# One stage for a row-wise linear layer and the normalisation behind it, in a twelve-sublayer network on one Trainium2 core

## The reference

```
def _ln(x, g, b):
    m = jnp.mean(x, -1, keepdims=True)
    v = jnp.var(x, -1, keepdims=True)
    return (x - m) * jax.lax.rsqrt(v + 1e-05) * g + b
...
    x_out = x + o @ li1_w + li1_b
    h = jax.nn.gelu(_ln(x_out, ln3_g, ln3_b) @ li2_w + li2_b, approximate=False)
    return x_out + h @ li3_w + li3_b
```

## Time and profile before

| what | us |
|---|---|
| median of 3 runs (4718.05 to 4733.04) | 4732.07 |
| profiled execution, its own time | 4727.11 |
| its span in the trace | 4725.3 |

### The profile page before, as it was taken

One profiled execution on the slowest core, in us unless ns is written; L12 is line 12 of the kernel. 1 busy time (PEld: TensorE's weight loads), 2 busy tenths in 40 slices (PEclk: granted clock), 3 DMA queues, 4 the chain that ended last, 5 costly groups with the idle time before them and its releaser, 6 DMA issues. The chain is left out here.

```text
span 4725.3 us, 108124 instructions
## 1 busy us (share of the span) xinstructions
PE 4236.6 (90%) x44572; PEld 3204.3 (68%) x44572; DVE 2559.6 (54%) x5119; ACT 1779.9 (38%) x3741; POOL 830.1 (18%) x532
## 2 busy tenths in 40 slices
PE   8889999999888989999977789886899999999987
PEld 5669889999666966666642379752699756666465
DVE  4268777777154045555529832246433466665454
ACT  2245555555121424444524312120244444445121
POOL 1122222221001200000019711005222100000300
PEclk9989999999988999999988889998899999999999
DMA  1010000000103931111012168649211100000100
GB/s 34 20 42 17 18 18 17 16 16 1 34 16 117 323 101 44 44 44 44 17 42 75 51 225 319 249 158 125 63 44 44 31 30 24 24 24 10 38 2 23
DMA packets 137848, 305.37 MB, mean 65 GB/s; under 512 B 51800, under 2 KB 87585, under 8 KB 119745
## 3 DMA queue, kind: packets, MB, share of 16 engines
q1 hardware_dynamic: 132992, 287.01, 19.5%
q0 software_dynamic: 4416, 12.06, 0.8%
HBM read 273.46 MB, written 23.47 MB: 63 GB/s over the span
## 5 line engine op out<-in xcount | busy, mean ns | idle before, releaser
L2850 DVE TENSOR_REDUCE block_max<-PS 128x1 f32<-128x512 f32 (+1 forms) x896 | 505.7, 627 | 300.4 <-PE PS L2710 299.8
L2799 ACT ACTIVATE probs_turned<-PS 128x512 f32<-128x512 f32 (+1 forms) x896 | 434.6, 571 | 562.1 <-PE PS L2731 562.0
L932 PE MATMUL PS<-context_turned,queries 128*128 128x422 f32 (+2 forms) x1536 | 336.8, 361 | 11.4 <-issue 8.3
L964 PE MATMUL PS<-probs_turned,context_part 128*128 128x256 f32 (+1 forms) x2496 | 331.8, 287 | 2.2 <-DVE weighted L1043 2.2
L993 ACT CAST probs_turned<-PS 128x512 fp32r<-128x512 f32 (+1 forms) x512 | 232.1, 510 | 238.8 <-PE PS L944 238.8
L1009 DVE TENSOR_TENSOR probs_turned<-PS,probs_turned 128x512 fp32r<-128x512 f32 (+1 forms) x512 | 276.6, 582 | 75.1 <-ACT probs_turned L993 73.2
L964 PEld LDWEIGHTS PS<-probs_turned,context_part 128*128 128x128 f32 (+1 forms) x2496 | 308.1, 189 | 2.4 <-DVE probs_turned L1009 2.4
L2751 PEld LDWEIGHTS PS<-probs_turned,values 128*17 128x17 f32 x13312 | 191.3, 97 | 149.3 <-issue 122.5
L932 PEld LDWEIGHTS PS<-context_turned,queries 128*128 128x128 f32 x1536 | 263.0, 191 | 40.0 <-issue 10.7
L129 PE MATMUL PS<-ident 128*128 128x256 f32 x850 | 233.7, 419 | 54.9 <-PEq L435 11.5
L2710 PE MATMUL PS<-keys_turned,queries 32*128 32x512 f32 (+1 forms) x2048 | 241.5, 548 | 40.7 <-ACT probs_turned L2799 35.5
(11 more groups left out here) (525 smaller groups left out, 7570.7 us busy)
## 6 DMA issues: line engine op xcount, KB each, us to landing
context_rows<-in_ctx SPq DMA_DIRECT2D x40, 768.0 KB
context_turned<-ctx_turned SPq DMA_DIRECT2D x32, 800.5 KB
routed_up<-in_L_ffn_W SPq DMA_DIRECT2D x23, 1024.0 KB
routed_down<-in_L_ffn_W SPq DMA_DIRECT2D x23, 1024.0 KB, 6.1
routed_up<-in_L_ffn_wg_w SPq DMA_DIRECT2D x23, 1024.0 KB
routed_second<-in_L_ffn_w_w SPq DMA_DIRECT2D x23, 1024.0 KB
routed_down<-in_L_ffn_w_w SPq DMA_DIRECT2D x23, 1024.0 KB, 5.2
v_all<-v_turned SPq DMA_DIRECT2D x128, 128.0 KB, 20.7
```

The lines of the kernel that those rows point to most:

```text
L932: last = nc.tensor.matmul(PS[:, j, 0:cols], qs[a][:, v, p * P:(p + 1) * P], yT[b][:, v, at:at + cols], start=(m == 0), stop=(m == 2))
L964: last = nc.tensor.matmul(O_ps, yp[a][0:kk, u, k, :], probsT[b][0:kk, par, k, :], start=(k == 0 and m == 0), stop=(k == KT - 1 and m == 2))
L2799: nc.scalar.activation(probs[0:kk, t % ring, i, 0:many].rearrange("p k c s -> p (k c s)"), PS[0:kk, bank_of("turned", t, i), 0:many * 2 * ...
L2850: nc.vector.tensor_reduce(part[:, b % 2, chunks[0]:chunks[-1] + 1, i, u // 2], bank, AX_X, ALU.max).then_inc(max_done.sem, 1)
```

## The change

`linear_rows` with the `normalize` behind it becomes one block, `linear_normal`. A sublayer no longer runs its last linear layer but returns it as a `Tail` (source, weights, destination, bases, bias), and the next one hands it to `begin`. In the new block the products, the addition and the statistics of a tile follow each other; variance, root and scaling go by groups of 4, 2 and 2 tiles; the first four tiles are turned behind the products of tile 5 (with two chunks, behind all products), the next two before, the last two after six spare products. All further bases are added by POOL, so `add` and the two `vector_steps` of layer 0's cross-attention go. The next sublayer's loads are issued at the start of this block. For that, what the tail still reads and what the next sublayer fills lie on two sides of SBUF, which `turn_side` swaps at each sublayer. The eviction of the turned banks and the order of the sublayers stay. The core of the diff:

```
+        return own.enter_context(self.nc.sbuf_tensor(f"{name}_{self.serial}", shape, dtype, side=self.side))
...
+def begin(core, tail, src, dst, **how):
+    if tail is None:
+        normalize(core, src, dst, **how)
+    else:
+        linear_normal(core, tail, dst, **how)
+        tail.own.close()
...
+    groups = (range(0, 4), range(4, 6), range(6, 8))
+    addends = tail.bases[1:] if tail.bias is None else [tail.bias] + tail.bases[1:]
...
+        with nc.Block() as block:
+            start_loads(core, block, loads, later)
+            @block.gpsimd
+            def _(pool):
+                if addends:
+                    tail.wait(pool)
+                for t in range(TILES):
+                    for n, more in enumerate(addends):
+                        if n:
+                            pool.wait_ge(based.sem, based.at(t * n_add + n))
+                        lead = addend if n else tail.bases[0]
+                        nc.gpsimd.tensor_tensor(addend[:, t, :], lead[:, t, :], more[:] if tail.bias is not None and n == 0 else more[:, t, :],
+                                                ALU.add).then_inc(based.sem, 1)
...
+                tail.wait(pe)
+                for t in range(TILES):
+                    for c in range(kc):
+                        last = nc.tensor.matmul(PS[:, t, 0:DIM], src[:, c, t * P:(t + 1) * P], w[:, c, 0:DIM],
+                                                start=(c == 0), stop=(c == kc - 1))
+                    last.then_inc(ready.sem, 1)
+                    if fills and t == (5 if kc >= 4 else TILES - 1):
+                        pe.wait_ge(step.sem, step.at(4 * per_tile))
+                        for f in range(DC):
+                            turn_tiles(f, groups[0]).then_inc(filled.sem, 1)
+                pe.wait_ge(step.sem, step.at(6 * per_tile))
+                if fills:
+                    for f in range(DC, 2 * DC):
+                        turn_tiles(f, groups[1])
+                spare_products(core, 4, 4)
+                pe.wait_ge(var_ready.sem, var_ready.at(len(groups)))
+                spare_products(core, 4, 2)
+                if fills:
+                    pe.wait_ge(step.sem, step.at(8 * per_tile))
+                    for f in range(DC, 2 * DC):
+                        turn_tiles(f, groups[2]).then_inc(filled.sem, 1)
...
+                nc.scalar.activation(warm[:], core.ident[0:1, 0:1], ACT.Sqrt)
+                deviation(0)
+                deviation(1)
+                if fills:
+                    if to_gain is not None:
+                        wait_weights(core, act)
+                    fill(0)
+                    fill(1)
+                deviation(2)
+                if fills:
+                    fill(3)
...
+                for t in range(TILES):
+                    if addends:
+                        dve.wait_ge(based.sem, based.at(n_add * (t + 1)))
+                    dve.wait_ge(ready.sem, ready.at(t + 1))
+                    nc.vector.tensor_tensor(X[:, t, :], PS[:, t, 0:DIM], addend[:, t, :], ALU.add).then_inc(summed.sem, 1)
+                    dve.wait_ge(summed.sem, summed.at(t + 1))
+                    nc.vector.bn_stats(stats[:, t, :], X[:, t, :]).then_inc(stats_done.sem, 1)
+                    for g, tiles in enumerate(groups[:-1]):
+                        if t == tiles[-1]:
+                            variance(g)
+                        if t == tiles[-1] + 1:
+                            scale(g)
+                variance(len(groups) - 1)
+                scale(len(groups) - 1)
...
-                    mlp(core, pre, R)
-                    add(core, U, U, R)
-                    normalize(core, U, U, ln["L0_xattn_ln2_g"], ln["L0_xattn_ln2_b"])
+        tail = mlp(core, work, pre, Tail(core, None, qT, w["li1_w"], R, [U], w["li1_b"]), U, [U])
+        linear_normal(core, tail, U, ln["L0_xattn_ln2_g"], ln["L0_xattn_ln2_b"])
...
-                        vector_steps(core, [lambda: nc.vector.tensor_tensor(R[:], R[:], U[:], ALU.add),
-                                            lambda: nc.vector.tensor_tensor(X[:], X[:], R[:], ALU.add)], 3)
+    return mlp(core, layer, pre, first, X, [U, X], [residual])
...
-        linear_rows(core, dtT, w["L1_attn_W_out"], X, None, X)
+    return Tail(core, hold, dtT, last["L1_attn_W_out"], X, [X])
```

More of the change, by code:

```diff
@@ L284, in normalize, with __init__, wait @@
     by_dve.passed(len(dve_fills))
+class Tail:
+    def __init__(self, core, own, src, w, dst, bases, bias=None):
+        self.own, self.src, self.w, self.dst, self.bases, self.bias = own, src, w, dst, bases, bias
+        self.landed, self.late = core.semaphore("weights_landed"), core.semaphore("late_weights_landed")
+        self.there, self.late_there = self.landed.past, self.late.past
+    def wait(self, eng):
+        eng.wait_ge(self.landed.sem, self.there)
+        if self.late_there:
+            eng.wait_ge(self.late.sem, self.late_there)
@@ new lines, in mlp @@
+def mlp(core, own, pre, tail, dst, bases, extra=[]):
+    shapes = {"ln3_g": [P, DC], "ln3_b": [P, DC], "li2_w": [P, DC, 4 * DIM], "li2_b": [P, 4 * DC],
+              "li3_w": [P, 4 * DC, DIM], "li3_b": [P, DIM]}
+    w = weights(core, own, pre, **shapes)
+    hat = core.sb(own, "hat", [P, TILES, DIM])
+    hatT = core.sb(own, "hat_turned", [P, DC, TOKENS])
+    inner = core.sb(own, "inner", [P, 4 * DC, TOKENS])
+    linear_normal(core, tail, hat, loads=w.loads + extra, turned=(hatT, w["ln3_g"], w["ln3_b"]))
+    linear_turned(core, hatT, w["li2_w"], inner, w["li2_b"], ACT.Gelu)
+    return Tail(core, own, inner, w["li3_w"], dst, [tail.dst] + bases, w["li3_b"])
@@ L3148, in l2_xattn @@
             uT = core.sb(front, "uT", [P, DC, TOKENS])
-            normalize(core, X, U, loads=w.loads, later=room.loads, turned=(uT, None, None))
+            begin(core, tail, X, U, loads=w.loads, later=room.loads, turned=(uT, None, None))
             linear_turned(core, uT, w["L2_xattn_Wq"], qT, w["L2_xattn_bq"])
@@ L3159, in l1_attn @@
     C = inner // P
+    core.turn_side()
+    hold = ExitStack()
+    last = weights(core, hold, L1_attn_W_out=[P, C, DIM])
+    dtT = core.sb(hold, "dtT", [P, C, TOKENS])
     with ExitStack() as own:
@@ L3173, in l1_attn @@
             kept = core.sb(front, "moments", [P, TILES, 2]), core.sb(front, "rstd", [P, 2, TILES])
-            normalize(core, X, U, loads=w.loads, turned=(uT, w["L1_attn_norm_w"], w["L1_attn_norm_b"]), twice=True, kept=kept)
+            begin(core, tail, X, U, loads=w.loads + last.loads, turned=(uT, w["L1_attn_norm_w"], w["L1_attn_norm_b"]), twice=True, kept=kept)
             linear_turned(core, uT, w["L1_attn_W_in"], zT, plain_of=(U, *kept))
@@ L3407, in l2_attn @@
         U = core.sb(own, "u", [P, TILES, DIM])
-        uT = core.sb(own, "uT", [P, DC, TOKENS])
         by_batch = lambda x: x[:].rearrange("p c (b s) -> p (c b) s", s=SEQ)
-        normalize(core, X, U, loads=w.loads, clear=firstT, turned=(uT, None, None))
+        begin(core, tail, X, U, loads=w.loads + last.loads, clear=firstT, turned=(uT, None, None))
         linear_turned(core, uT, w["L2_attn_v_w"], vT)
@@ L3651, in l3_attn @@
                 uT = core.sb(front, "uT", [P, DC, TOKENS])
-                normalize(core, X, U, loads=w.loads + q_loads, later=late_loads, turned=(uT, w["L3_attn_ln_gamma"], w["L3_attn_ln_beta"]), twice=True)
+                begin(core, tail, X, U, loads=w.loads + last.loads + q_loads, later=late_loads, turned=(uT, w["L3_attn_ln_gamma"], w["L3_attn_ln_beta"]), twice=True)
                 for n, x in enumerate((qT, kT)):
@@ L3659, in l3_attn, with l3_ffn @@
         turn(core, V, C, qT)
-        linear_rows(core, qT, w_out, X, w["L3_attn_b_out"], X)
-def l3_ffn(core):
+    return Tail(core, hold, qT, w_out, X, [X], last["L3_attn_b_out"])
+def l3_ffn(core, tail):
     heads, d = 8, 32
@@ L3681, in l3_ffn @@
         kept = core.sb(own, "moments", [P, TILES, 2]), core.sb(own, "rstd", [P, 2, TILES])
-        normalize(core, X, hat, loads=w.loads + masks.loads, turned=(uT, w["norm_w"], w["norm_b"]), twice=True, kept=kept)
+        begin(core, tail, X, hat, loads=w.loads + masks.loads, turned=(uT, w["norm_w"], w["norm_b"]), twice=True, kept=kept)
         def cut(c):
```

335 lines of the change are left out of this document (225 added, 110 removed).

## The result

| | before | after |
|---|---|---|
| median of the runs compared on one chip | 4728.79 us (4 runs, 4718.05 to 4733.04) | 4625.04 us (4 runs, 4619.05 to 4627.87) |
| the profiled execution (span) | 4727.1 us (4725.3) | 4627.87 us (4626.1) |
| forecast | | 4663 us, range 4646 to 4684 |

The ratio is 0.978 (95% interval 0.9762 to 0.9797): 103.75 us faster. The direction is the forecast's, the size is not: 68.9 us had been expected, and the time lies 21 us under the low end of the range. In a second set of runs on another chip the same kernel took 4623.53 us (ratio 0.9785, 0.9758 to 0.9812).

The account below looks back on a forecast made before the run. Row-wise linear stages were taken as bound by TensorE, normalisations by VectorE, one behind the other at ten places. Overlap 45.3 + loads 15.3 + slow restarts 8.3 = 68.9 us, so 4732.07 - 68.9 = 4663 us, range 4646 to 4684.

Parts of the forecast that it names:

- Overlap, tile by tile: At ten places, normalisation work runs beside the linear stage's multiplies instead of behind them: 45.3 us gained.
- the four kinds: Merged stages, first multiply to next stage: four chunks 20.8 us, two 15.15, eight with turns 33.15, eight without turns 31.8.
- DMA waits: Evictions scaled by a gain from memory wait for late-issued loads at five places; early issue removes 15.3 us.
- Loads: Next stage's weights issued at the linear stage's start: stalls of 15.3 us and slow restarts of 8.3 go, together 23.6.
- Slow restarts: Multiplies after DMA waits start at the lower clock; without the waits 8.3 us are gained at four places.
- the 2.3: Slow-restart gain at one place: 64 multiplies take 30.20 us against 2 x 13.97 at full clock.
- POOL: POOL adds bias and all bases under the multiplies: cost nothing, statistics not slowed; far end 38 us.
- No fall of the clock in the short stages: Clock holds through TensorE's new pauses in two- and four-chunk stages; rival that it falls, costing 10 to 25 us: 0.14.
- the length of the longest pause: Reason for no clock fall: longest new pause 2.0 us, nearest to 1.84, which stayed fast; 2.97 ran slow.
- the prediction's reading of the Trainium skill: A loop whose multiplies wait for data each round can be throttled anew; this favours the falling-clock rival (0.14), 10 to 25 us.
- The failed step: Claimed nothing outside the ten stretches (305.25 us, 6.5% of the span) gains, except the clock at the start of what follows.

Follow-up runs that it names:

- split: The kernel after with every linear stage and normalisation again a block of its own, loads issued in the normalisation; 4731.68 us, ratio 1.0003.
- split_early: As split, but the next layer's loads are issued at the start of the linear block; 4708.02 us, ratio 0.9953.
- no_spares: The kernel after without the six spare products ahead of the last transposes in each merged stage; 4681.42 us.
- before_shorter_end: The kernel before without its last feed-forward sublayer, so the program ends earlier; whole time not compared, scan 124.0 us.
- after_shifted: The kernel after with 22 tiny multiplies (88 instructions) in the opening block, moving the code behind them; 4656.32 us, ratio 0.9862.
- before_shifted: The kernel before with 39 one-element multiplies (156 instructions) in the opening block, moving the code behind them; 4757.65 us, ratio 1.0076.
- before_shift43: The kernel before with 43 one-element multiplies in the opening block, 16 instructions more than before_shifted; 4722.37 us, ratio 0.9957.

## Why the prediction was right in its steps and wrong in its sum

- *Overlap, tile by tile.* Right: stage lengths within 0.15 us of the forecast in the four kinds. Overlap and DMA waits together 61.5 against 60.6.
- *Loads.* Right in kind, and measured by itself: 27.6 us at the five places in the traces of split and split_early, 23.6 forecast; that the medians differ by 23.7 is luck, as said above. No DMA wait ahead of a scaled eviction is left.
- *Slow restarts.* 9.0 against 8.3: two of them, taken as 1.5 and 1.4, were 1.7 each, and the 2.3 was 2.5. One more gain of the clock was not foreseen: it fell inside the router's 32 multiplies before (4.60 us) and falls only behind them after (3.92).
- *POOL.* Right: it is now busy for 5.5 to 17.1 us of a stretch, beside the multiplies, and the statistics beside it take 0.43 where 0.41 had been taken. POOL is not the reason, they take 0.43 in the two-chunk stretch without it too (1391.15).
- *No fall of the clock in the short stages.* Right: 1.00 in the two-chunk stretch with its pause of 1.81 us. But the reason given, the length of the longest pause, does not carry it: no_spares has no pause above 1.92 us at this place either, and its clock fell (0.50 behind the stage). The six spare products were costed as 2.6 us that lengthen the list; they are what holds the clock. By the prediction's reading of the Trainium skill (TensorE: Matmul & The Clock Gate, HAM oscillation) the short stages would have been throttled; with the spares they were not (1.00). The waits that this section tells of last some 3 to 5 us, longer than any pause here, so neither trace tests it.
- *The failed step* is the sentence "Nothing outside can gain from the change, apart from the clock at the start of what follows." Two pieces of work outside gained.

The first is the loop's code. With the ratios to the kernel before as the measure, a kernel before whose loop lies well is worth 4728.79 x 0.9957 = 4708.4 us, so 20 of the 103.75 us (15 to 26 by the interval) are to be had without the change at all; the change got them since it shortened the code ahead of the loop by 87 instructions. This hangs on one set of runs; in the profiled pair, with two refetching trips before, the loop's part is 12.6. The second is the scan, 13 us. 68.9 + 20 + 13 = 102, or with the loop of the profiled pair 68.9 + 12.6 + 13 = 94.5; the rest is scattered.

As a mechanism of the loop this is shown: code moved, and nothing else, switches the refetching on in one kernel (none to five trips) and off in the other (one to three trips to none). The Trainium skill (Runtime: NRT & Kernel Launch, Instruction fetch mechanics) says that TensorE's instruction memory holds 128 KiB, refilled in blocks of 16 KiB. That is eight blocks, and by it seven touched ones and one fetched ahead just fit. The trace agrees in the size of a packet and in that seven stay. The same section also says that a taken branch to code outside the current two pages stalls; here a jump back over 6.7 pieces fetches nothing in seven programs (0 or 1 packets in the whole stretch, 4.6 us of such waits in all), so the measurement speaks against that for TensorE. That the eighth block is taken by the piece fetched ahead is argued from the page's figure, not shown. That the boundary lies 0.05 to 0.10 of a piece behind my count is inferred from where the loop refetches; that eight pieces refetch in one to three trips in the kernel before, five in split, and in none in before_shorter_end isn't explained.

What makes the scan's transfers faster stays open. Shown is only what it isn't: the address of its source within the scratch tensors (2, 20 and 128 KB), the length of TensorE's program, the first or the second half of the merging alone, the spares, and the state of the loop. All six programs with ten merged places had it at 108 to 111.3 us and 147 to 151 GB/s, all twelve others at 119 to 126.4 and 127 to 136. The absolute places of code and tensors in the device's memory were not to be seen or chosen.

## What to carry to other kernels

Where a stage bound by TensorE is followed by one bound by VectorE, lay them beside each other tile by tile, start the next stage's loads in it, and keep spare multiplies in TensorE's pauses; this could be worked out from rows (68.9 for 70.5 us). Before you credit a change with a gain, compare the traces outside the place where it was made: a loop of six trips whose code is 6.7 pieces long gained or lost 10 to 40 us here by the number of instructions ahead of it, and the code-load queue's packets inside the loop tell so at once. Such a loop is worth placing on purpose.

## What the runs showed of the hardware that was not expected

- Code of a loop of 6.7 pieces of 16,384 bytes is kept from trip to trip or fetched again (9 packets a trip), depending on as little as 16 instructions ahead of it; a refetching trip costs 4.5 us with one pause (after_shifted) and 7.7 with two (before_shifted against before_shift43).
- The same 128 transfers with all DMA engines busy run at 133 GB/s in one program and at 149 in another, through the whole scan and again in a second profiled execution of each (134 and 147).
- Six spare products of 0.43 us in a stage of 15 us decide whether the next stage starts at a granted clock of 0.50, though no pause at that place is longer than 1.92 us without them.
